# PE's waits put in front of a projection's last matmul, and one ACT copy put ahead of the third exponentials

## The chip, the cores and the metric

The kernel runs on one core of one Trainium2 chip. The metric is the device time of one execution in microseconds (us). Its engines are PE (TensorE, matmuls; PEld is its weight load), DVE (VectorE), ACT (ScalarE), POOL (GpSimd) and SP (SyncE, which issues the DMAs here). Each has its own queue of instructions and waits for the others by semaphores.

## What is computed

A transformer-like block on x of 4 x 512 x 256: a state-space mixer and a gated feed-forward part, each behind a modulated layer norm. The mixer is what matters here; cut to it, the reference is:

```python
proj = u @ W_in.T                                # u: 4 x 512 x 256
xBC, z, A_log = split(proj)                      # x: 256, B and C: 32 heads x 64 each
xBC = causal_conv(xBC, conv_w, 4 taps) + conv_b
x, Bm, Cm = split(xBC)
a = -softplus(A_log)
Lm = exp(segsum(a))                              # 512 x 512 per head, lower triangle
M = einsum('blhn,bshn,bhls->bhls', Cm, Bm, Lm)
y = einsum('bhls,bshp->blhp', M, x) + D * x
out = (y * silu(z + z_bias)) @ W_out.T
```

After it come the gate and residual, the second layer norm, silu(x W1) * (x W3), a Walsh-Hadamard transform folded into W2, and the product with W2.

## The kernel before

The 32 heads are taken in 8 groups of 4, and each group over the 4 batches: 32 steps (g, b). The sequence of 512 is cut into 4 chunks of 128. Inside a chunk M is built directly; between chunks the kernel carries states. A step projects four tiles t = 0 to 3 of 128 channels: t = 0, 1 are B, t = 2, 3 are C (each two pairs of heads). A projection is 6 matmuls of 128 x 512 on the full 128x128 array: weights and inputs are split in a high and a low part, so there are three products (lines 371 to 373) for each of two halves of the depth.

The steps are software-pipelined, and the order on each engine is written out by hand. In PE's step (g, b), b is the batch that is projected, q the step before it, r the step before that:

- `proj` 1 (B of b), `states` of r (48 matmuls of 128x32, line 566), `scores` of r for the second head pair (32 of 64x64, line 547), `b_transposes` of q (3 of 128x128, line 528);
- `proj` 0, `proj` 3, `proj` 2;
- `inter` of r (the earlier states' y parts, 12 matmuls of 128x32, line 583), `intra` of r (the chunk's own y, 32 of 128x32, line 597), `scores` of q for the first pair, `b_transposes` of q for the second.

Each of these helpers holds its semaphore waits at its own head, so the waits for `states` stand behind `proj` 1 and those for `inter` behind `proj` 2.

ACT's step is: copy the states out (line 874), exponentials 0 and 1 of q (line 865, four instructions each), the first tap of the convolution for tiles 1 and 0 out of PSUM (line 831), in batch 3 two casts of the next group's weights (lines 914, 915), exponentials 2, then `b_evacuate(q, 0)` (line 855, which copies the B transposes out of PSUM into b_tok), the taps of tiles 3 and 2, the copy of y (line 880), in batch 3 small coefficient copies (line 931), `b_evacuate(q, 1)` and exponentials 3. In batch 1 a copy (line 940) stands ahead of the exponentials. The taps of tiles 3 and 2 wait for `intra` of r on PE.

DVE's step is six further taps for tiles 1 and 0 (line 1174), the mix (scores times exponentials, line 1162) of q's first pair, six taps for tiles 3 and 2, the mix of the second pair. POOL masks the running sums (line 1475), scales x for the states (line 1448) and splits weights (line 1396). SP loads the running sums (line 234) for each head after the exponentials have used the ones before, and stores y.

Semaphores by name: `taps0` to `taps3` count finished taps of a tile, `bt` transposes, `bt_ev` the copies of line 855 (two a step), `xds_done` the scaled x, `st_copy` the states copied out, `yt_ev` the copy of y, `xs_done` x for `intra`, `mixed` the mixes, `proj0` to `proj3` finished projections. `pe_waits` is only incremented, so that an instruction carries the waits before it. The loop over groups 1 to 7 is a loop on the chip; the steps of group 0 are written out.

Of the kernel before, what the change touches and what calls it, by code (L numbers as in the profile page):

```python
# [19 lines left out]
B, L, D = 4, 512, 256  # L20
# [3 lines left out]
KT = D // P  # L24
# [26 lines left out]
def adaln_ssm_ffn_kernel(nc, u, w_bc, w_x, w_a, w_z, conv, d_rows, z_bias, w_out, w13, w2, c_t, wmod,  # L51
                         consts, out, e_d, gates_d):
    with ExitStack() as ctx:
# [312 lines left out]
        def _(pe):  # L366
# [99 lines left out]

            def proj(g, b, t):
                n = g * B + b
                if isinstance(n, int) and n == 0:
                    pe.wait_ge(s[f"xtaps{t % 2}"], 3 * (3 + t // 2))  # L470
                else:
                    pe.wait_ge(s[f"taps{t}"], 3 * n)
                if b == 0:
                    pe.wait_ge(s["w_split"], g * GT + PLACE[t] + 1)
                for kt in range(KT):
                    i = split_mm(ps[:, PROJ_BANK[t], :], wg_hi[:, t, kt, :], wg_lo[:, t, kt, :],
                                 ht_hi[:, kt, b * L:(b + 1) * L], ht_lo[:, kt, b * L:(b + 1) * L],
                                 kt == 0, kt == KT - 1)
                i.then_inc(s[f"proj{t}"], 1)

# [40 lines left out]
            def b_transposes(q, b, p, first):  # L521
                pe.wait_ge(s[f"taps{p}"], 3 * q + 3)
                if not first or p:
                    pe.wait_ge(s["bt_ev"], 2 * q + p)
                if not first and p == 0:
                    pe.wait_ge(s["st_copy"], 2 * q)
                for c in range(CH - 1):
                    i = nc.tensor.transpose(ps[:, 6, c * P:(c + 1) * P],  # L528
                                            acc[:, b % 2, p, c * P:(c + 1) * P], ident)
                i.then_inc(s["bt"], 1)  # L530

            def scores(q, b, p, first):
# [5 lines left out]
                else:  # L538
                    pe.wait_ge(s["xtok_ev"], 2 * B)
                pe.sem_inc(s["pe_waits"], 1)  # L540
                for c in range(CH):
                    for h in range(2):
# [11 lines left out]
            def states(q, b):  # L554

                pe.wait_ge(s["bt_ev"], 2 * q + 2)
                pe.wait_ge(s["xds_done"], 3 * q + 3)
                pe.sem_inc(s["pe_waits"], 1)
                for p in range(2):
                    for c in range(CH - 1):  # L560
# [11 lines left out]
            def inter(q, b, first):  # L572

                pe.wait_ge(s["st_copy"], 2 * q + 2)
                if first:
                    pe.wait_ge(s["gate_ev"], 1)
                else:
                    pe.wait_ge(s["yt_ev"], q)
                for c in (2, 1, 3):
                    for p in range(2):  # L580
# [5 lines left out]
            def intra(q, b):  # L586

                pe.wait_ge(s["xs_done"], 4 * q + 4)
                pe.wait_ge(s["mixed"], 2 * q + 2)
                for a in range(2):  # L590
                    for h in range(2):
# [34 lines left out]
            def step(g, b, gq, gr):  # L626
# [3 lines left out]
                r = gr * B + br  # L630
                proj(g, b, 1)
                states(r, br)
                scores(r, br, 1, False)
                b_transposes(q, bq, 0, False)
                proj(g, b, 0)
                proj(g, b, 3)
                proj(g, b, 2)
                inter(r, br, isinstance(r, int) and r == 0)
                intra(r, br)
                scores(q, bq, 0, False)  # L640
                b_transposes(q, bq, 1, False)

# [105 lines left out]
        def _(act):  # L748
# [145 lines left out]
            def step(g, b, gq, gr, split=False, last=False):  # L894
# [17 lines left out]
                if split:  # L912
                    act.wait_ge(s["ld_wg"], (g + 2) * 16)
                    nc.scalar.copy(wg_hi[:, 1], wg_raw[:, 1]).then_inc(s["w_high_act"], 1)
                    nc.scalar.copy(wg_hi[:, 0], wg_raw[:, 0]).then_inc(s["w_high_act"], 1)
                decays(q, bq, 2, False)
                b_evacuate(q, 0)
                last_tap(g, b, 3)
# [737 lines left out]
```

## Time and profile before

| | us |
|---|---|
| median of 3 runs | 542.92 (542.3 to 543.33) |
| the profiled execution | 542.52 |
| its span | 540.3 |

| engine | busy, share of the span |
|---|---|
| PE | 529.2 us, 98% |
| PEld | 428.9 us, 79% |
| DVE | 455.4 us, 84% |
| ACT | 373.8 us, 69% |
| POOL | 240.7 us, 45% |

All comes from one profiled execution, with times in us from the start of its span; the granted TensorE clock is 0.999 of full speed over it, that is 2.4 GHz. A matmul's end in the records is modelled and longer than the time for which it holds the array, so distances are read from start to start. An instruction's idle time stands in brackets with what ended it; "issue" means that the profile shows nothing that it waited for. The scan with its 32 steps lies between about 49 and 363 us; before it come the first layer norm and the decays, behind it the feed-forward part.

### The profile page before, as it was taken

How to read it: one execution, taken by the hardware profiler on the slowest of the kernel's cores; microseconds unless marked ns; L12 is line 12 of the kernel's file. 1: busy time of each engine (PE TensorE's matmuls, PEld its weight loads, DVE VectorE, ACT ScalarE, POOL GpSimd, SP SyncE). 2: the span in 40 equal slices, each digit the busy share in tenths (PEclk: the TensorE clock that was granted, in tenths of full speed). 3: DMA queues.
4: the chain of work that ended last, by engine and by line, in shares of the span. 5: the costliest groups of instructions: out<-in, count | busy, mean ns of one | idle time of the engine just before them, and what ended most of it. 6: DMA issues, size and time to landing. Idle time of an engine off the chain costs nothing.

```text
span 540.3 us, 19200 instructions
## 1 busy us (share of the span) xinstructions
PE 529.2 (98%) x7091; PEld 428.9 (79%) x7092; DVE 455.4 (84%) x746; ACT 373.8 (69%) x988; POOL 240.7 (45%) x465
## 2 busy tenths in 40 slices
PE   7899999999999999999999999999999999999997
PEld 4577778878878878878878878876889889889886
DVE  6999999999999999999999999999757657657342
ACT  1878998888898898898898898887534234234240
POOL 6763366676676775776776474374000000000000
PEclk9999999999999999999999999999999999999999
DMA  8737333432423425422422424666521322100101
GB/s 265 279 111 225 111 121 90 138 92 84 139 84 91 139 86 168 139 81 93 138 80 96 137 80 135 168 183 197 170 79 41 78 79 79 39 2 0 40 0 40
DMA packets 50288, 59.38 MB, mean 110 GB/s; under 512 B 8004, under 2 KB 44740, under 8 KB 49864
## 3 DMA queue, kind: packets, MB, share of 16 engines
q1 hardware_dynamic: 50248, 58.88, 35.4%
q8 instruction: 21, 0.34, 0.3%
q14 instruction: 19, 0.16, 0.1%
HBM read 48.75 MB, written 9.05 MB: 107 GB/s over the span
## 4 chain that ended last, share of the span: by engine, by line
PE 87%; DVE 7%; ACT 2%; issue 2%; DMA 1%; POOL 1%; SPq 1%; ACTq 0%; POOLq 0%; DVEq 0%
PE ps L371 20%; PE ps L372 19%; PE ps L373 19%; PE ps L547 9%; PE ps L528 5%; DVE acc L1174 4%; PE ps L597 4%; PE ps L566 3%; PE ps L583 3%; PE ps L664 3%; DMA u_sb<-in_u 1%; PE ps L610 1%; PE ps L674 1%; DVE stats L1050 1%; ACT decay L865 1%
## 5 line engine op out<-in xcount | busy, mean ns | idle before, releaser
L1174 DVE SCALAR_TENSOR_TENSOR acc<-ps,cw_dve,acc 128x511 f32<-128x511 f32 (+2 forms) x384 | 257.9, 742 | 5.1 <-ACT acc L831 4.8
L865 ACT ACTIVATE decay<-sums,p_slot 128x128 f32<-128x128 f32 (+1 forms) x512 | 147.7, 371 | 2.9 <-ACT p_slot L940 1.2
L1475 POOL TENSOR_TENSOR sums<-sums,far_above 128x256 f32<-128x256 f32 x128 | 95.6, 752 | 118.4 <-DMA sums<-packed_sums 112.2
L831 ACT ACTIVATE acc<-ps,cw_act 128x512 f32<-128x512 f32 x128 | 93.1, 777 | 27.3 <-PE ps L597 25.2
L371 PE MATMUL ps<-ht_hi,wg_hi 128*128 128x512 f32 x256 | 107.1, 418 | 0.4 <-POOL wg_lo L1396 0.4
L372 PE MATMUL ps<-ht_lo,wg_hi 128*128 128x512 f32 x256 | 101.2, 395 | 0.0
L373 PE MATMUL ps<-ht_hi,wg_lo 128*128 128x512 f32 x256 | 101.2, 395 | 0.0
L1000 ACT ACTIVATE silu_sb<-ps 128x512 f32<-128x512 f32 x32 | 19.2, 600 | 77.7 <-PE ps L373 77.7
L1162 DVE TENSOR_TENSOR mix<-ps,decay 128x768 f32<-128x768 f32 x64 | 61.0, 954 | 5.6 <-PE ps L547 4.8
L1401 POOL TENSOR_TENSOR rstd<-vareps,minus_half 128x4 f32<-128x4 f32 x8 | 8.4, 1048 | 118.7 <-DVE vareps L1056 116.4
L547 PE MATMUL ps<-acc 64*64 64x128 f32 (+1 forms) x2048 | 57.6, 249 | 0.8
L373 PEld LDWEIGHTS ps<-ht_hi,wg_lo 128*128 128x128 f32 x256 | 48.1, 188 | 11.6
L371 PEld LDWEIGHTS ps<-ht_hi,wg_hi 128*128 128x128 f32 x256 | 48.2, 188 | 10.1 <-POOL wg_lo L1396 0.9
L1313 DVE TENSOR_TENSOR hid<-ps,silu_sb 128x512 f32<-128x512 f32 x32 | 22.1, 692 | 40.4 <-ACT silu_sb L1000 40.3
L372 PEld LDWEIGHTS ps<-ht_lo,wg_hi 128*128 128x128 f32 x256 | 48.5, 189 | 8.4
L547 PEld LDWEIGHTS ps<-acc 64*64 64x64 f32 x2048 | 48.8, 133 | 7.1 <-issue 2.2
L371 PE MATMUL ps<-h_hi,w_hi 128*128 128x512 f32 x128 | 50.5, 394 | 0.0
L373 PE MATMUL ps<-h_hi,w_lo 128*128 128x512 f32 x128 | 49.9, 390 | 0.0
L372 PE MATMUL ps<-h_lo,w_hi 128*128 128x512 f32 x128 | 49.9, 390 | 0.0
L371 PE MATMUL ps<-w_hi,hid_hi 128*128 128x256 f32 x128 | 36.9, 289 | 0.2 <-DVE stage L1329 0.2
L372 PE MATMUL ps<-w_lo,hid_hi 128*128 128x256 f32 x128 | 36.2, 283 | 0.0
L373 PE MATMUL ps<-w_hi,hid_lo 128*128 128x256 f32 x128 | 36.2, 283 | 0.0
(143 smaller groups left out, 892.8 us busy)
## 6 DMA issues: line engine op xcount, KB each, us to landing
sums<-packed_sums SPq DMA_DIRECT2D x256, 96.0 KB, 2.7
wg_raw<-in_w_bc SPq DMA_DIRECT2D x8, 512.0 KB, 4.1
y_parts<-yt_sb SPq DMA_DIRECT2D x64, 64.0 KB, 2.0
stage<-y_parts SPq DMA_DIRECT2D x32, 128.0 KB, 2.8
u_sb<-in_u SPq DMA_DIRECT2D x4, 512.0 KB, 5.0
stage<-in_w SPq DMA_DIRECT2D x1, 2048.0 KB, 14.2
x_channels<-acc SPq DMA_DIRECT2D x8, 256.0 KB, 2.4
ee<-running_sums SPq DMA_DIRECT2D x8, 256.0 KB
```

The source lines that it names most:

```text
L371: mm(o, w_hi, x_hi, start=first, stop=False)
L372: mm(o, w_hi, x_lo, start=False, stop=False)
L373: return mm(o, w_lo, x_hi, start=False, stop=last)
L528: i = nc.tensor.transpose(ps[:, 6, c * P:(c + 1) * P], acc[:, b % 2, p, c * P:(c + 1) * P], ident)
L547: i = mm(ps[NS * at:NS * (at + 1), 2 + a, o:o + P - NS * h], acc[own, b % 2, p, c * P + NS * h:c * P + NS * (h + 1)], acc[own, b % 2, 2 + ...
L597: i = mm(ps[QD * quarter:QD * (quarter + 1), 7, k * P + NS * h:(k + 1) * P], xs[:, b % 2, w:w + QD], mix[:, j, k * PW + NS * (1 - h):k * P ...
L831: af(acc[:, b % 2, t, :], ps[:, PROJ_BANK[t], :], ACT.Identity, bias=cw_act[:, t, 1:2], scale=cw_act[:, t, 0:1]).then_inc(s[f"tap_a{t}"], 1)
L865: i = af(decay[:, j, own], sums[:, j, own], ACT.Exp, scale=-1.0, bias=p_slot[:, b * CH + n, j:j + 1])
L1162: tt(mix[:, 2 * p:2 * p + 2, 0:PL], ps[:, 2:4, 0:PL], decay[:, 2 * p:2 * p + 2, 0:PL], ALU.mult).then_inc(s["mixed"], 1)
L1174: stt(a[:, d:], ps[:, PROJ_BANK[t], 0:L - d], cw_dve[:, t, TAPS - 1 - d:TAPS - d], a[:, d:], ALU.mult, ALU.add).then_inc(s[f"taps{t}"], 1)
L1313: tt(hid[:, m % 2, :], ps[:, 2 + m % 2, :], silu_sb[:, m % 2, :], ALU.mult).then_inc(s["hid_done"], 1)
L1475: gp.tensor_tensor(v, v, far, ALU.add).then_inc(s["masked"], 1)
```

## The change

On PE, `proj` is cut in two: `proj_start` issues the waits of the projection and its first five matmuls, `proj_end` the sixth. In the steps that have r and q (all but the first two), the waits that stood at the heads of `states`, of the first `scores` (without `mixed`) and of the first `b_transposes` (without `st_copy`) now stand between `proj_start(g, b, 1)` and `proj_end(b, 1)`; of those of `inter`, `intra`, the second `scores` and the second `b_transposes` all that are not implied by others stand between `proj_start(g, b, 2)` and `proj_end(b, 2)`. The matmuls, their order and their operands stay; so do the conditions, each of which is waited for no later in the queue than before. Two increments of `pe_waits` a step go. On ACT, `b_evacuate(q, 0)` moves from behind to ahead of the exponentials 2. The first two steps and the stretch after the loop keep the old form.

```diff
-            def proj(g, b, t):
+            def proj_start(g, b, t):
...
-                for kt in range(KT):
-                    i = split_mm(ps[:, PROJ_BANK[t], :], wg_hi[:, t, kt, :], wg_lo[:, t, kt, :],
-                                 ht_hi[:, kt, b * L:(b + 1) * L], ht_lo[:, kt, b * L:(b + 1) * L],
-                                 kt == 0, kt == KT - 1)
-                i.then_inc(s[f"proj{t}"], 1)
+                o, own = ps[:, PROJ_BANK[t], :], slice(b * L, (b + 1) * L)
+                split_mm(o, wg_hi[:, t, 0, :], wg_lo[:, t, 0, :], ht_hi[:, 0, own], ht_lo[:, 0, own], True, False)
+                mm(o, wg_hi[:, t, 1, :], ht_hi[:, 1, own], start=False, stop=False)
+                mm(o, wg_hi[:, t, 1, :], ht_lo[:, 1, own], start=False, stop=False)
+
+            def proj_end(b, t):
+
+                own = slice(b * L, (b + 1) * L)
+                mm(ps[:, PROJ_BANK[t], :], wg_lo[:, t, 1, :], ht_hi[:, 1, own], start=False,
+                   stop=True).then_inc(s[f"proj{t}"], 1)
...
-                proj(g, b, 1)
-                states(r, br)
-                scores(r, br, 1, False)
-                b_transposes(q, bq, 0, False)
+                proj_start(g, b, 1)
+                pe.wait_ge(s["xds_done"], 3 * r + 3)
+                pe.wait_ge(s["taps3"], 3 * r + 3)
+                pe.wait_ge(s["taps1"], 3 * r + 3)
+                pe.wait_ge(s["taps0"], 3 * q + 3)
+                pe.wait_ge(s["bt_ev"], 2 * r + 2)
+                proj_end(b, 1)
+                states_now(br)
+                pe.wait_ge(s["mixed"], 2 * r + 1)
+                pe.sem_inc(s["pe_waits"], 1)
+                scores_now(br, 1)
+                pe.wait_ge(s["st_copy"], 2 * r + 2)
+                b_transposes_now(bq, 0)
                 proj(g, b, 0)
                 proj(g, b, 3)
-                proj(g, b, 2)
-                inter(r, br, isinstance(r, int) and r == 0)
-                intra(r, br)
-                scores(q, bq, 0, False)
-                b_transposes(q, bq, 1, False)
+                proj_start(g, b, 2)
+                if isinstance(r, int) and r == 0:
+                    pe.wait_ge(s["gate_ev"], 1)
+                else:
+                    pe.wait_ge(s["yt_ev"], r)
+                pe.wait_ge(s["xs_done"], 4 * r + 4)
+                pe.wait_ge(s["taps2"], 3 * q + 3)
+                pe.wait_ge(s["taps1"], 3 * q + 3)
+                pe.wait_ge(s["mixed"], 2 * r + 2)
+                pe.wait_ge(s["bt_ev"], 2 * q + 1)
+                proj_end(b, 2)
+                inter_now(br)
+                intra_now(br)
+                scores_now(bq, 0)
+                b_transposes_now(bq, 1)
...
+                b_evacuate(q, 0)
                 decays(q, bq, 2, False)
-                b_evacuate(q, 0)
                 last_tap(g, b, 3)
```

## Rows read from the trace of the kernel before

**Rows 1.** The page, part 1: busy us (share of the span) and instructions.

```profile
PE 529.2 (98%) x7091; PEld 428.9 (79%) x7092; DVE 455.4 (84%) x746; ACT 373.8 (69%) x988; POOL 240.7 (45%) x465
```

**Rows 2.** Timeline of PE and PEld, batch 3: start, duration, instruction, count, [idle before].

```profile
311.37 0.40 PE L373 MATMUL ps<-ht_hi,wg_lo 128*128 128x512 f32 x1
317.49 0.39 PE L373 MATMUL ps<-ht_hi,wg_lo 128*128 128x512 f32 x1
...
311.14 0.19 PEld L373 LDWEIGHTS ps<-ht_hi,wg_lo 128*128 128x128 f32 x1
311.70 0.51 PEld L566 LDWEIGHTS ps<-xds,b_tok 128*32 128x32 f32 x48 [0.37 <-issue]
317.81 0.25 PEld L583 LDWEIGHTS ps<-acc,st_sb 128*32 128x32 f32 x10 [0.36 <-issue]
```

**Rows 3.** Line 589's wait, and timeline of PEld at other changes of work.

```profile
L589 PEldq EVENT_SEMAPHORE  x2: 51/51/51, 316.4 to 326.6; - x2
...
27.38 0.14 PEld L423 LDWEIGHTS ps<-h,wa_sb 128*32 128x32 f32 x4 [0.36 <-issue]
...
54.36 0.48 PEld L528 LDWEIGHTS ps<-cst,acc 128*128 128x128 f32 x3
```

**Rows 4.** Timeline of ACT's second b_tok copies, and PE in the first step.

```profile
310.74 0.50 ACT L855 COPY b_tok<-ps 128x384 f32<-128x384 f32 x1
320.88 0.50 ACT L855 COPY b_tok<-ps 128x384 f32<-128x384 f32 x1
58.59 0.48 ACT L855 COPY b_tok<-ps 128x384 f32<-128x384 f32 x1
...
58.93 0.40 PE L373 MATMUL ps<-ht_hi,wg_lo 128*128 128x512 f32 x1
```

**Rows 5.** Timeline of two copies on ACT and the weight loads that waited for them.

```profile
332.99 0.20 ACT L874 COPY st_sb<-ps 64x48 f32<-64x48 f32 x1
333.31 0.31 PEld L528 LDWEIGHTS ps<-cst,acc 128*128 128x128 f32 x3
...
80.47 0.43 ACT L874 COPY st_sb<-ps 64x48 f32<-64x48 f32 x2 [0.19 <-PE ps L566]
81.08 0.20 PEld L528 LDWEIGHTS ps<-cst,acc 128*128 128x128 f32 x2
```

**Rows 6.** Timeline of PE and PEld in a step of batch 0.

```profile
320.14 0.19 PEld L371 LDWEIGHTS ps<-ht_hi,wg_hi 128*128 128x128 f32 x1
320.48 0.39 PE L372 MATMUL ps<-ht_lo,wg_hi 128*128 128x512 f32 x1
321.41 0.40 PE L373 MATMUL ps<-ht_hi,wg_lo 128*128 128x512 f32 x1
321.73 0.51 PEld L566 LDWEIGHTS ps<-xds,b_tok 128*32 128x32 f32 x48 [0.37 <-issue]
322.39 0.69 PEld L547 LDWEIGHTS ps<-acc 64*64 64x64 f32 x30
```

**Rows 7.** Timeline of ACT's third exponentials, and of projection 2's last matmul on PE.

```profile
317.12 1.18 ACT L865 ACTIVATE decay<-sums,p_slot 128x128 f32<-128x128 f32 x4
75.49 1.18 ACT L865 ACTIVATE decay<-sums,p_slot 128x128 f32<-128x128 f32 x4
75.06 0.39 PE L373 MATMUL ps<-ht_hi,wg_lo 128*128 128x512 f32 x1
296.89 1.17 ACT L865 ACTIVATE decay<-sums,p_slot 128x128 f32<-128x128 f32 x4
297.42 0.39 PE L373 MATMUL ps<-ht_hi,wg_lo 128*128 128x512 f32 x1
```

**Rows 8.** Timeline of PE where a projection starts late.

```profile
77.98 0.50 PE L371 MATMUL ps<-ht_hi,wg_hi 128*128 128x512 f32 x1
118.95 0.51 PE L371 MATMUL ps<-ht_hi,wg_hi 128*128 128x512 f32 x1 [0.39 <-POOL wg_lo L1396]
```

**Rows 9.** Timeline of DVE's taps of tiles 1 and 0.

```profile
305.98 4.02 DVE L1174 SCALAR_TENSOR_TENSOR acc<-ps,cw_dve,acc 128x511 f32<-128x511 f32 x6
```

More of the change, by code:

```diff
@@ L474, in proj @@
                     pe.wait_ge(s["w_split"], g * GT + PLACE[t] + 1)
-                for kt in range(KT):
-                    i = split_mm(ps[:, PROJ_BANK[t], :], wg_hi[:, t, kt, :], wg_lo[:, t, kt, :],
-                                 ht_hi[:, kt, b * L:(b + 1) * L], ht_lo[:, kt, b * L:(b + 1) * L],
-                                 kt == 0, kt == KT - 1)
-                i.then_inc(s[f"proj{t}"], 1)
+                o, own = ps[:, PROJ_BANK[t], :], slice(b * L, (b + 1) * L)
[6 more added lines that the diff above has]
+                   stop=True).then_inc(s[f"proj{t}"], 1)
+            def proj(g, b, t):
+                proj_start(g, b, t)
+                proj_end(b, t)
             pe.wait_ge(s["zero_set"], 1)
@@ L526, in b_transposes, with b_transposes_now @@
                     pe.wait_ge(s["st_copy"], 2 * q)
+                b_transposes_now(b, p)
+            def b_transposes_now(b, p):
                 for c in range(CH - 1):
@@ L540, in scores, with scores_now @@
                 pe.sem_inc(s["pe_waits"], 1)
+                scores_now(b, p)
+            def scores_now(b, p):
                 for c in range(CH):
@@ L558, in states, with states_now @@
                 pe.sem_inc(s["pe_waits"], 1)
+                states_now(b)
+            def states_now(b):
                 for p in range(2):
@@ L578, in inter, with inter_now @@
                     pe.wait_ge(s["yt_ev"], q)
+                inter_now(b)
+            def inter_now(b):
                 for c in (2, 1, 3):
@@ L589, in intra, with intra_now @@
                 pe.wait_ge(s["mixed"], 2 * q + 2)
+                intra_now(b)
+            def intra_now(b):
                 for a in range(2):
```

## The prediction

> **What bounds the kernel now.** I read the page's busy shares first: PE is busy for 98% of the span, DVE for 84%, ACT for 69% [rows 1]. PE sets the pace, so I went to the timeline of PE and its weight loads in the middle of the scan, where one step (one group of heads, one batch) takes 10.03 us: the loads of the states begin at 311.70 and again at 321.73 [rows 2, 6]. Inside a projection a long matmul starts every 0.23 us, and its weights are loaded beside the matmul before it: those of the matmul of 311.37 from 311.14 on [rows 2]. At two places of a step this breaks. After the last matmul of projection 1 the states' load starts 0.33 us later, and after the last of projection 2 (317.49) the load for the earlier states' y parts 0.32 us later, each with 0.36 or 0.37 us of idle time marked "issue" [rows 2]. So some 0.09 us lies open twice a step. With 30 steps that have states, at most 0.09 x 60 = 5.4 us could come back there.
>
> **Is that opening the price of the waits?** I say no, by two readings. One: the wait on line 589, which stands before the y parts, was executed at 316.4, over 1 us before 317.81, and the opening is there all the same [rows 2, 3]. Two: before the B transposes of 54.36 stands a wait as well, yet their load carries no idle mark; they use the full 128x128 array, as the projections do. The loads of 128x32 at 27.38 have one wait in front and carry the mark of 0.36 us, the same as the states with two waits and a semaphore increment [rows 2, 3]. The opening goes with the change from the full array to a part of it, and that stays. So I book no gain, with 5.4 us as the other bound. The Trainium skill (TensorEngine Tiling (Array Packing), Key Properties) says that a change of tiling mode drains TensorE. By that rule too the opening stays and the sum is as below; without it the sum would be 5.4 us lower. The rows on both shapes agree with it, though none shows the drain itself.
>
> **What the moved waits ask for.** In front of the last projection matmul they must be met 0.3 to 0.6 us sooner. Most are early: DVE has finished the taps of the batch before at 305.98 + 4.02 = 310.00, needed at 311.14 [rows 2, 9]; the second mix, POOL's scaled x and the y copy of the batch before are earlier by 1 us or more, and cost nothing. Two are late, and both are ACT's copy of transposes to b_tok. Queued behind the waiting load on PE is everything: the last projection matmul, states, scores, transposes. ACT's last tap waits for that matmul, DVE's taps and mix for ACT. A delay isn't won back on ACT, whose next copy hangs on taps that wait for the end of PE's y parts.
>
> **The price of a late wait.** From the end of a copy on ACT to the load that waits for it: 332.99 + 0.20 = 333.19 to 333.31, so 0.12 us [rows 5]. From a load that nothing covered to streaming: the load starts at 320.14, the second matmul after it is recorded at 320.48, and the first must have begun to stream 0.23 us before that, at 320.25: 0.11 us [rows 6]. Together 0.23 us from the end of the copy. The bounds: the copy that ended at 80.47 + 0.43 = 80.90 was followed by its load at 81.08, 0.18 instead of 0.12, which makes 0.29; and if the weights were in the array already, 0.12 alone is left [rows 5].
>
> **Part A, the waits before projection 1's last matmul.** The copy begun at 310.74 ends at 311.24; that matmul can stream at 311.47 instead of 311.37, 0.10 us late [rows 2, 4]. Of the 30 steps 22 are of this kind: 2.2 us. In steps of batch 0 ACT has one small copy more before it (line 931) and ends at 320.88 + 0.50 = 321.38, so 321.61 instead of 321.41: 0.20 us, five times, and once 0.10: 1.1 us; the seventh is held by weights before that and pays nothing [rows 4, 6]. These seven give something back. Scores follow states after 0.66 us there (321.73 to 322.39), 0.10 more than in other steps, because three waits are handled between them after a late release, and two of the three move forward: 0.7 us off [rows 6]. The first step costs 58.59 + 0.48 + 0.23 = 59.30 against 58.93: 0.37 us [rows 4]. Semaphore increments dropped I take as nothing; PE's queue hides them. A = 2.2 + 1.1 - 0.7 + 0.4 = 3.0 us.
>
> **Part B, the waits before projection 2's last matmul, with ACT's moved copy.** The copy now starts where the third exponentials started, and takes 0.46 to 0.48 us, so streaming is possible 0.69 us after that start. In steps of batches 0 and 2 the start is early enough by 0.27 us or more, and that is nothing. Batch 3: two weight casts (lines 914, 915) stand ahead on ACT, in seven steps: 317.12 + 0.69 = 317.81 against 317.49, 0.32 us, five times, so 1.6 us; where ACT had also waited for POOL, 75.49 + 0.69 = 76.18 against 75.06, 1.12 us; once 0.46 us. Together 3.2 us [rows 2, 7]. Batch 1: a copy (line 940) stands ahead: 296.89 + 0.69 = 297.58 against 297.42, 0.16 us, five like it 0.8 us and two others 0.3 us: 1.1 us [rows 7]. B = 4.3 us. The exponentials come 0.38 us later. What hides that is ACT's idle time before its next tap, 0.5 to 1.1 us in most steps; without it up to 0.4 us a step would go to DVE's taps.
>
> **What swallows part of it.** In the step before 120 PE already waits 0.39 us for POOL's weight split at 118.95, and about as much again in starting up; that hides the 0.32 of the step before. At 77.98 PE starts a projection some 0.25 us late, held by DVE, which hides as much of the 1.12 [rows 8]. The last step of the scan is bound by DVE: 0.1. Together 0.7 us.
>
> **The sum.** 3.0 + 4.3 - 0.7 = 6.6 us. The profiled execution took 542.52 us (span 540.3 and 2.2 around it), so 549.1 for one like it. It stands 0.4 under the median of the runs, 542.92, which becomes 549.5.
>
> **Rivals.**
> - *Stalls dearer.* In other steps too the blocked sequencer falls behind, and short matmuls after it start late, as in batch 0 by 0.10 us [rows 6]. Against it: the release is followed by one long matmul, which gives it time. In 23 steps and at 14 places of part B: 37 x 0.10 = 3.7 more, 553.2.
> - *The openings were the waits', the stalls as priced.* For it: the page calls them "issue" [rows 2]. Against it: the two readings. 549.5 - 5.4 = 544.1.
> - *Faster.* The openings go, and a held last matmul has its weights in already, so a late wait costs 0.12 and not 0.23. Part A: 0.3 for the first step, 5 x 0.09 for batch 0, less 0.7: 0. Part B: 5 x 0.21 + 1.01 + 0.35 + 0.4 = 2.8. Sum 0 + 2.8 - 0.5 - 5.4 = -3.1: 539.8. The place is the pair of openings in each step; it decides once they return more per step than the two stalls take. Against it: the loads that waited for a copy start only after its end [rows 5].
> - *It does not bite.* The copies land in time, because ACT gains elsewhere, and nothing opens or closes: 542.9. For it: the margins are a tenth of a us. Against it: ACT's time is tied to PE's.
>
> **How the numbers follow.** Forecast 0.62, stalls dearer 0.10, openings gone with the stalls as priced 0.13, faster 0.07, no effect 0.08. Bounds of the forecast: 43 stalls (29 in A, 14 in B), each by 0.06 more or 0.10 less: 545.2 to 552.1. To leave out no more than 2 in 10 the range takes in the first two rivals: 543.8 to 553.2. About 0.2%, or 1.1 us, is what a measurement of this kernel can tell from no change. The second rival ends at that bound and is split. Faster 0.08, same 0.12, slower 0.80.
>
> **What would show it.** Right: the idle marks before states and y parts stay at 0.32 to 0.37 us; the last weight load of projection 1 starts 0.12 us after ACT's b_tok copy ends and no longer beside its forerunner; from the states of batch 3 to the next states 10.5 us, from batch 2's to batch 3's 10.13. Wrong: states 0.23 us after the last long matmul, steps of 10.03 us as before, or the copy of line 855 ending well ahead of the last matmul of projection 1 or 2.

## The result, and the profile after

| kernel | median (lowest to highest) | runs |
|---|---|---|
| before | 542.52 us (541.85 to 543.54) | 9 |
| changed | 546.27 us (544.55 to 548.52) | 9 |

The ratio is 1.0072, with an interval of 1.0058 to 1.0086: slower by 3.75 us, where 6.6 were forecast. The profiled execution of the changed kernel has a span of 543.8 us, 3.5 more than before.

The page after, part 1 (engines) and the row of the granted clock of part 2. They answer [rows 1].

```profile
PE 533.5 (98%) x7092; PEld 429.1 (79%) x7092; DVE 455.8 (84%) x746; ACT 373.2 (69%) x988; POOL 240.6 (44%) x465
PEclk9899999999999999999999999999999999999999
```

DVE, ACT and POOL do what they did; only PE's busy time moves, by 4.3 us. The 8 near the start is a dip of the clock ahead of the scan that some executions of a kernel show and others don't, so stretches are compared here and not only spans.

In the changed kernel the last projection matmul is line 483, states 585, scores 563, y parts 605 (`inter`) and 622 (`intra`), the b_tok copy 899. The waits by engine and line after: us in total, times, longest.

```profile
PEld ps L483 <- ACT b_tok L899: 10.8, 40, 0.6
PEld ps L605 <- issue: 9.9, 32, 0.6
PEld ps L585 <- issue: 7.7, 31, 0.4
```

The first line is the new wait: 40 of some 60 last matmuls are held by ACT's copy, as forecast (43). The 10.8 us are idle time of the weight loader, not of the array: a load may stand late and still lie beside the matmul before it. The two other lines are the openings, which are still there.

Timeline after of PEld, PE and ACT, steps of batches 2 and 3. They answer [rows 2, 4, 7]. A view marks idle time from 0.15 us on.

```profile
309.48 0.19 PEld L478 LDWEIGHTS ps<-ht_lo,wg_hi 128*128 128x128 f32 x1
309.72 0.19 PEld L483 LDWEIGHTS ps<-ht_hi,wg_lo 128*128 128x128 f32 x1
310.27 0.26 PEld L605 LDWEIGHTS ps<-acc,st_sb 128*32 128x32 f32 x10 [0.36 <-issue]
...
313.79 0.19 PEld L483 LDWEIGHTS ps<-ht_hi,wg_lo 128*128 128x128 f32 x1 [0.19 <-ACT b_tok L899]
314.21 0.51 PEld L585 LDWEIGHTS ps<-xds,b_tok 128*32 128x32 f32 x48 [0.24 <-issue]
...
320.15 0.19 PEld L483 LDWEIGHTS ps<-ht_hi,wg_lo 128*128 128x128 f32 x1 [0.48 <-ACT b_tok L899]
320.57 0.25 PEld L605 LDWEIGHTS ps<-acc,st_sb 128*32 128x32 f32 x10 [0.24 <-issue]
...
324.19 0.19 PEld L483 LDWEIGHTS ps<-ht_hi,wg_lo 128*128 128x128 f32 x1 [0.28 <-ACT b_tok L899]
324.61 0.51 PEld L585 LDWEIGHTS ps<-xds,b_tok 128*32 128x32 f32 x48 [0.24 <-issue]
...
313.64 0.40 PE L478 MATMUL ps<-ht_lo,wg_hi 128*128 128x512 f32 x1
313.87 0.42 PE L483 MATMUL ps<-ht_hi,wg_lo 128*128 128x512 f32 x1
314.22 0.60 PE L585 MATMUL ps<-xds,b_tok 128*32 128x24 f32 x48
...
319.71 0.39 PE L478 MATMUL ps<-ht_lo,wg_hi 128*128 128x512 f32 x1
...
313.24 0.50 ACT L899 COPY b_tok<-ps 128x384 f32<-128x384 f32 x1
...
319.01 0.40 ACT L958 CAST wg_hi<-wg_raw 128x256 fp32r<-128x256 f32 x1
319.62 0.48 ACT L899 COPY b_tok<-ps 128x384 f32<-128x384 f32 x1
...
323.64 0.50 ACT L899 COPY b_tok<-ps 128x384 f32<-128x384 f32 x1
```

Three kinds of place are to be seen. At 309.72 (projection 2, batch 2) nothing is late: the load stands 0.24 behind its forerunner, as in a plain projection. At 313.79 (projection 1) the copy ended at 313.74 and the load follows it by 0.05 us, early enough to lie beside the matmul of 313.64, which streams until 313.87; the last matmul's record is at 313.87, and PE loses nearly nothing. At 320.15 (projection 2, batch 3) the matmul before ended its streaming at 319.94, the load has no cover, and the y parts come at 320.57 instead of 320.26.

A step is best read from states to states. The medians over the steps of one batch, worked out from the first record of each of the 32 groups of states, and the means, which hold the irregular steps too:

| from the states in the step that projects batch | 0 | 1 | 2 | 3 |
|---|---|---|---|---|
| steps | 7 | 7 | 8 | 8 |
| before, median (mean) | 10.13 (10.13) | 10.03 (10.05) | 10.03 (10.04) | 10.05 (10.37) |
| after, median (mean) | 10.03 (10.03) | 10.13 (10.15) | 9.99 (10.00) | 10.49 (10.68) |

By the means, 7 x -0.10 + 7 x 0.10 + 8 x -0.03 + 8 x 0.31 = 2.2 us. Half of the steps are shorter than before, which the forecast had nowhere; the loss is in the column of batch 3. A stretch runs into the next step, so that column holds what projection 1 of batch 0 loses too.

The rest of the 3.5 us lies outside. The first states wait for ACT's first copy; and behind the scan stands a gap that before does not have. Timeline after, ACT and PEld, in the first step, and PEld at the y parts of the tail; the last line is before's tail:

```profile
58.77 0.50 ACT L899 COPY b_tok<-ps 128x384 f32<-128x384 f32 x1
59.38 0.19 PEld L483 LDWEIGHTS ps<-ht_hi,wg_lo 128*128 128x128 f32 x1 [0.53 <-issue]
59.81 0.51 PEld L585 LDWEIGHTS ps<-xds,b_tok 128*32 128x32 f32 x48 [0.24 <-issue]
...
380.15 0.36 PEld L605 LDWEIGHTS ps<-acc,st_sb 128*32 128x32 f32 x10
381.09 0.14 PEld L605 LDWEIGHTS ps<-acc,st_sb 128*32 128x32 f32 x2 [0.58 <-issue]
...
377.38 0.36 PEld L583 LDWEIGHTS ps<-acc,st_sb 128*32 128x32 f32 x12
```

From the end of the first copy to the first states it is 59.81 - 59.27 = 0.54 us; before, the copy of 58.59 ended at 59.07 [rows 4] and the states came at 59.26, 0.19: 0.35 more. In the tail, 12 loads that need no wait between them stand in a row at 377.38 in before; after, they break behind the tenth for 0.58 us.

All kernels in one table, by stretches of their traces. The middle one, from the first states to the last, is the scan without its first step. The last, from the last states to the span's end, holds the break. Each ratio is taken to runs of before from the same round, whose medians are 542.39 to 542.76, so it can differ a little from the quotient of the times shown.

| kernel | us, median | ratio to before (interval) | first states at | scan | behind it |
|---|---|---|---|---|---|
| before | 542.52 | | 59.26 | 315.41 | 165.6 |
| changed | 546.27 | 1.0072 (1.0058 to 1.0086) | 59.81 | 317.59 | 166.4 |
| e1_a_only | 542.17 | 0.9995 (0.9985 to 1.0004) | 59.61 | 314.37 | 166.7 |
| e2_b_only | 546.81 | 1.0077 (1.0061 to 1.0093) | 61.07 | 317.64 | 166.1 |
| e3_bt_behind | 541.92 | 0.9985 (0.9971 to 0.9999) | 60.26 | 313.58 | 167.0 |
| e4_act_old | 573.32 | 1.0566 (1.0540 to 1.0591) | 60.07 | 344.65 | 166.0 |
| e5_casts_behind | 543.73 | 1.0018 (1.0006 to 1.0029) | 59.03 | 315.18 | 166.6 |
| e6_taps_only | 540.87 | 0.9965 (0.9954 to 0.9976) | 59.44 | 312.95 | 165.7 |
| e7_bt_behind_pad | 542.37 | 1.0001 (0.9991 to 1.0011) | 61.74 | 312.61 | 165.6 |
| e8_transposes_first | 544.77 | 1.0048 (1.0028 to 1.0068) | 60.80 | 317.69 | 165.5 |
| e9_bt_first | 548.81 | 1.0105 (1.0090 to 1.0120) | 59.83 | 320.83 | 166.1 |

### The profile page after: what moved, and what is told of

It is laid out like the page before. It is cut to its first block, busy times and chain, and to the rows that moved or that the text cites. A ratio compares the mean times of both kernels' runs of the same rounds, so it can differ in the third digit from the quotient of the medians.

```text
span 543.8 us, 19055 instructions
## 1 busy us (share of the span) xinstructions
PE 533.5 (98%) x7092; PEld 429.1 (79%) x7092; DVE 455.8 (84%) x746; ACT 373.2 (69%) x988; POOL 240.6 (44%) x465
## 4 chain that ended last, share of the span: by engine, by line
PE 88%; ACT 4%; DVE 4%; issue 2%; DMA 1%; POOL 0%; SPq 0%; ACTq 0%; DVEq 0%; POOLq 0%
PE ps L371 15%; PE ps L372 14%; PE ps L373 14%; PE ps L563 8%; PE ps L483 6%; PE ps L541 5%; PE ps L478 5%; PE ps L477 5%; PE ps L622 4%; PE ps L585 3%; PE ps L605 3%; PE ps L708 3%; DVE acc L1218 2%; ACT decay L909 1%; DMA sums<-packed_sums 1%
## 5 line engine op out<-in xcount | busy, mean ns | idle before, releaser
L483 PE MATMUL ps<-ht_hi,wg_lo 128*128 128x512 f32 x128 | 53.1, 415 | 1.2 <-ACT b_tok L899 0.7
L373 PE MATMUL ps<-ht_hi,wg_lo 128*128 128x512 f32 x128 | 50.5, 394 | 0.0
L483 PEld LDWEIGHTS ps<-ht_hi,wg_lo 128*128 128x128 f32 x128 | 24.1, 188 | 16.4 <-ACT b_tok L899 10.8
```

Of the source, the lines that this page charges most:

```text
L373: return mm(o, w_lo, x_hi, start=False, stop=last)
L483: mm(ps[:, PROJ_BANK[t], :], wg_lo[:, t, 1, :], ht_hi[:, 1, own], start=False, stop=True).then_inc(s[f"proj{t}"], 1)
```

## The experiments

**The two halves, each alone (e1, e2).** e1 changes projection 1's group only and leaves ACT as before:

```diff
-                proj(g, b, 1)
-                states(r, br)
-                scores(r, br, 1, False)
-                b_transposes(q, bq, 0, False)
+                proj_start(g, b, 1)
+                pe.wait_ge(s["xds_done"], 3 * r + 3)
+                pe.wait_ge(s["taps3"], 3 * r + 3)
+                pe.wait_ge(s["taps1"], 3 * r + 3)
+                pe.wait_ge(s["taps0"], 3 * q + 3)
+                pe.wait_ge(s["bt_ev"], 2 * r + 2)
+                proj_end(b, 1)
...
                 proj(g, b, 2)
                 inter(r, br, isinstance(r, int) and r == 0)
```

e2 is the reverse: projection 2's group and ACT's moved copy as in the change, projection 1's group as before.

> Only the first half of PE's change: the waits before states, the first scores and the first B transposes stand before the last matmul of projection 1; projection 2 and ACT's order are as in the kernel before. Late-copy theory, priced from the trace of the changed kernel: in ordinary steps the last matmul's load starts 0.05 us after the copy to b_tok and costs the step 0.02 us, while the scores follow the states 0.05 us sooner; batch 0 loses 0.13 and gets 0.11 back, the first step loses 0.3. Sum about -0.4, so 542.1 beside 542.5, no measurable change. Rival, part A as the prediction had it (0.10 a step, 3.0 in all): 545.5. Rival, the openings were the waits': states 0.23 us after the last long matmul, 3 us less.

> Only the second half: the waits before the y parts stand before the last matmul of projection 2 and ACT copies the transposes ahead of the third exponentials; projection 1 as before. Late-copy theory: batch 3 loses 0.32 us five times, 0.45 once and about 0.9 once, batch 1 loses 0.13 five times and 0.3 once: +4.0, so 546.5, nearly all of the change's loss. Rival, the loss is spread over both halves as predicted (4.3 minus 0.6 here, 3.0 in the other): 546.2 here and 545.5 for the other half. Rival, a general slowing by the longer wait list: batches 0 and 2 would lose too.

Waits of e1, then of e2 (the line of the b_tok copy is 889 and 890 in them):

```profile
PEld ps L483 <- ACT b_tok L889: 5.9, 28, 0.3
...
PEld ps L483 <- ACT b_tok L890: 4.6, 13, 0.6
```

e1 holds 28 loads, each for a short time, and costs nothing: 0.9995. e2 holds 13, and is as slow as the whole change. Its batches 1 and 3 take 10.12 and 10.38 us (medians), the others 10.12 and 10.03 as before. So the loss is the second half's. By the medians of the runs the halves add up: 0.9995 x 1.0077 = 1.0072. In the traces, of which there is one for each kernel, they don't quite: in the scan e1 is 1.04 us shorter than before, and the changed kernel is 3.22 longer than e1, while e2 is 2.23 longer than before. Irregular steps make much of that difference of 1.0. In the first step of batch 3, where POOL holds ACT, it is 0.46: 10.29 us in before and 10.62 in e2, but 10.09 in e1 and 10.88 after. The second step of batch 3 adds 0.57 and the last takes 0.52 off again. That the second half has less to hide behind where the first has removed a hold-up would explain the first two; no run shows it.

**Only the b_tok waits behind, ACT as before (e3).** From the changed kernel:

```diff
-                pe.wait_ge(s["bt_ev"], 2 * r + 2)
                 proj_end(b, 1)
+                pe.wait_ge(s["bt_ev"], 2 * r + 2)
                 states_now(br)
...
-                pe.wait_ge(s["bt_ev"], 2 * q + 1)
                 proj_end(b, 2)
                 inter_now(br)
                 intra_now(br)
                 scores_now(bq, 0)
+                pe.wait_ge(s["bt_ev"], 2 * q + 1)
                 b_transposes_now(bq, 1)
...
-                b_evacuate(q, 0)
                 decays(q, bq, 2, False)
+                b_evacuate(q, 0)
```

> The change without the two waits for b_tok copies: they stand behind the projections again, one directly before states, one before the second B transposes, and ACT has its old order; all other waits stay moved. Late-copy theory: no load of a last matmul waits any more; what stays is the return between states and scores, 0.05 us in 22 steps and 0.11 in 7: -2.0, so 540.5, faster than both kernels. The openings before states and y parts stay at 0.32 to 0.33 us, before the y parts with no wait at all in between. Rival, openings due to waits: 3 to 5 us less, 537 to 540. Rival, the moved waits themselves cost: 544 or more.

The scan is 1.83 us shorter than before, but the time only 0.6 (540.5 was expected). PEld in e3's tail:

```profile
376.62 0.36 PEld L605 LDWEIGHTS ps<-acc,st_sb 128*32 128x32 f32 x11
378.19 0.11 PEld L605 LDWEIGHTS ps<-acc,st_sb 128*32 128x32 f32 x1 [1.22 <-issue]
```

The break took the gain: 1.22 us, now behind the eleventh load. The y parts, which in this kernel have no wait and no increment between them and the last long matmul, still come 0.32 us behind it (0.318 to 0.325 in all 30 steps). All waits that are met in time cost nothing; the two b_tok waits are the loss.

**The break moved away (e7).** e3 with 48 increments of `pe_waits` more on PE ahead of the scan. Nothing in the scan or in the tail is different.

```diff
             norm_transposes(0)
+            for _ in range(24):
+                pe.sem_inc(s["pe_waits"], 1)
...
             norm_transposes(2)
+            for _ in range(24):
+                pe.sem_inc(s["pe_waits"], 1)
```

> The version with the b_tok waits left behind the projections, and 48 semaphore increments on PE in two idle stretches of the first layer norm, so that the code behind the scan lies where it lay in the kernel before. Theory of code loading: the break of 0.4 to 1.2 us among the twelve y-part matmuls behind the scan goes, and the scan's 1.8 us reach the end: 540.7. Rival, the break has another cause (data or PSUM): 541.9 as without them, or a little more for the increments.

PEld in e7's tail:

```profile
377.11 0.36 PEld L609 LDWEIGHTS ps<-acc,st_sb 128*32 128x32 f32 x12
```

The break is gone, and behind the scan the trace has 165.6 us, as before. The time was a miss, 542.37 for 540.7, and alone it would speak for the rival: the padding stands in front of work of PE, and in e7's trace the scan's first long matmul comes at 41.34 instead of 39.11 us, with the clock's dip in that stretch. In the traces of e2, e3, e4, e8 and e9, which have the dip and no padding, it comes at 39.43 to 40.43, which leaves 0.9 to 1.9 us for the padding, an estimate.

What the run shows is that the break hangs on where the instructions stand in PE's program. The other kernels say it more sharply. Counted in the compiled programs, where each y part is two instructions, a load and a matmul:

| kernel | PE's program, instructions more or less than before's | the break stands ahead of | idle, us |
|---|---|---|---|
| e1 | -10 | load 3 of 12 | 1.07 |
| e2 | -12 | load 4 | 0.51 |
| e9 | -23 | matmul 9, load 10 | 0.54 |
| after, e4, e5 | -26 | load 11 | 0.58, 0.40, 0.85 |
| e3 | -28 | load 12 | 1.22 |
| e6, e8, before, e7 | -6, -3, 0, +20 | no break | |

In all seven traces with a break it falls on the same place of the program. In e1, for one, the y parts begin 10 instructions sooner than in before and four of them stand ahead of load 3, so the break lies 6 instructions ahead of where before's y parts begin; 12 - 6, 26 - 20, 28 - 22, and 23 - 17 for e9's matmul 9, give 6 as well. In e6 that place is the first y part, in the three others it lies among the scores.

And the traces show what arrives there. The page has a DMA queue for instructions, q8, with 21 packets, 0.34 MB; that is about the size of PE's program (348 KB) in pieces of 16 KB. In each of the seven a piece landed 1.25 to 1.48 us before the break ended (after: landed at 379.75, the break ended at 381.09; e3: 376.79 and 378.19). In the four without a break the same piece had landed 2.8 to 3.5 us before the first y part (before: 373.93 for 377.38; e7: 373.98 for 377.11). So in the break PE waits for the next piece of its program, by all that the timing can tell. Why the piece starts 3.9 to 4.7 us before the first y part in the four, and only 1.0 to 2.0 us before it once the program is 10 or more instructions shorter, isn't shown.

**ACT's order (e4).** The changed kernel with `b_evacuate(q, 0)` back behind `decays(q, bq, 2, False)`.

```diff
-                b_evacuate(q, 0)
                 decays(q, bq, 2, False)
+                b_evacuate(q, 0)
```

> PE's part of the change whole, but ACT copies the transposes behind the third exponentials as before. Late-copy theory: the last load of projection 2 starts 0.05 us after the end of that copy in every step, some 0.7 us late in batches 0 and 2, 1.1 in batch 1 and 1.3 in batch 3: about +25, 566 to 572. Rival, ACT's move is not what the time hangs on: 546.

The wait of e4, and ACT and PEld in its timeline:

```profile
PEld ps L483 <- ACT b_tok L899: 39.3, 56, 1.7
...
310.08 0.46 ACT L899 COPY b_tok<-ps 128x384 f32<-128x384 f32 x1
310.60 0.19 PEld L483 LDWEIGHTS ps<-ht_hi,wg_lo 128*128 128x128 f32 x1 [0.96 <-ACT b_tok L899]
```

27.1 us more in the scan than after, 0.9 a step, and a time just above the 566 to 572 that were expected: without the moved copy every step's last matmul of projection 2 waits for four exponentials. Nearly nothing of a late copy is won back elsewhere, since ACT's next taps wait for PE in turn: in batch 3 the last matmul of projection 2 and the y parts behind it come 1.37 us late (1.50 us behind the matmul before, and 0.42 behind the record, for 0.23 and 0.32), and the step takes 11.45 us instead of before's 10.05, 1.40 more. That is the loop that the forecast assumed.

**The casts of batch 3 (e5).** The changed kernel with the copy ahead of the two weight casts too:

```diff
+                b_evacuate(q, 0)
                 if split:
                     act.wait_ge(s["ld_wg"], (g + 2) * 16)
                     nc.scalar.copy(wg_hi[:, 1], wg_raw[:, 1]).then_inc(s["w_high_act"], 1)
                     nc.scalar.copy(wg_hi[:, 0], wg_raw[:, 0]).then_inc(s["w_high_act"], 1)
-                b_evacuate(q, 0)
                 decays(q, bq, 2, False)
```

> The changed kernel with one more move on ACT: in batch 3 the two weight casts stand behind the copy to b_tok instead of ahead of it. Late-copy theory: the copy starts 0.6 us sooner in batch 3, so the last matmul of projection 2 is no longer held there (0.32 us five times, 0.45 and up to 0.9 once): 2.5 to 3 less than the changed kernel, 543.5 beside 542.5 for the kernel before; batch 1 keeps its 0.13. Rival, the loss comes from the list of waits as such: 546 as the changed kernel.

ACT and PEld of e5 in a step of batch 3:

```profile
316.13 0.48 ACT L899 COPY b_tok<-ps 128x384 f32<-128x384 f32 x1
316.49 0.42 ACT L959 CAST wg_hi<-wg_raw 128x256 fp32r<-128x256 f32 x1
...
316.82 0.19 PEld L483 LDWEIGHTS ps<-ht_hi,wg_lo 128*128 128x128 f32 x1
317.37 0.25 PEld L605 LDWEIGHTS ps<-acc,st_sb 128*32 128x32 f32 x10 [0.36 <-issue]
```

The load is no longer held, and batch 3 takes 10.09 us (median) instead of 10.49. The scan is 2.4 us shorter than after's: two casts ahead of one copy were most of the loss, 2.5 of 3.75 us by the medians of the runs.

**Is the opening the change of array shape? (e8).** In before, the B transposes, which use the full array as the projection does, are put directly behind projection 1, ahead of states and scores:

```diff
                 proj(g, b, 1)
+                if not (isinstance(r, int) and r == 0):
+                    pe.wait_ge(s["st_copy"], 2 * r)
+                b_transposes(q, bq, 0, True)
                 states(r, br)
                 scores(r, br, 1, False)
-                b_transposes(q, bq, 0, False)
```

> The kernel before with one order changed on PE: the first B transposes, on the full array, stand directly behind projection 1, and states and scores behind them; the waits in front of the transposes are three, one of them the late copy to b_tok. Array-shape theory: the transposes' load starts beside or within 0.05 us of the end of the last long matmul (0.23 to 0.28 us after its start, no idle mark or a small one), and the opening moves to between transposes and states. Rival, waits make the opening: the transposes start 0.33 us or more after the last long matmul, as states did. The time itself within 2 us of the kernel before.

PEld and PE of e8 behind projection 1 (line 373 is its last matmul, 528 the transposes, 566 the states):

```profile
314.11 0.19 PEld L373 LDWEIGHTS ps<-ht_hi,wg_lo 128*128 128x128 f32 x1
314.34 0.48 PEld L528 LDWEIGHTS ps<-cst,acc 128*128 128x128 f32 x3
314.99 0.51 PEld L566 LDWEIGHTS ps<-xds,b_tok 128*32 128x32 f32 x48 [0.17 <-issue]
...
314.34 0.39 PE L373 MATMUL ps<-ht_hi,wg_lo 128*128 128x512 f32 x1
314.57 0.49 PE L528 MATMUL ps<-cst,acc 128*128 128x128 f32 x3
```

Behind the same projection, with three waits in front of them, the transposes' load starts beside the last long matmul, with no idle mark, and their first matmul follows at the plain 0.23 us. The mark has moved to the states, where the shape changes now. With e3, where no wait is left and the opening stays, that settles it: the opening goes with the shape. It agrees with the rule of the Trainium skill that a change of tiling mode drains TensorE (TensorEngine Tiling (Array Packing), Key Properties); the price, some 0.09 us from a matmul of 512 columns on the full array to 128x32, is this trace's. Behind short matmuls a change of shape shows less: the loads lie 0.05 to 0.09 us apart from states to scores, from y parts to scores and from scores to transposes, and 0.17 from transposes to states here. The kernel as a whole is slower by 0.5%, or 2.2 us, a little more than the 2 expected; the likely reason is that ACT's copies of the states now come later (e8's waits have ACT idle for states for 16.7 us, before's for 2.9), which no run separates.

**The price of a late wait, by its place in the group (e9).** The changed kernel with the late wait first of the five in projection 1's group instead of last:

```diff
                 proj_start(g, b, 1)
+                pe.wait_ge(s["bt_ev"], 2 * r + 2)
                 pe.wait_ge(s["xds_done"], 3 * r + 3)
                 pe.wait_ge(s["taps3"], 3 * r + 3)
                 pe.wait_ge(s["taps1"], 3 * r + 3)
                 pe.wait_ge(s["taps0"], 3 * q + 3)
-                pe.wait_ge(s["bt_ev"], 2 * r + 2)
                 proj_end(b, 1)
```

> The changed kernel with one change of order: in front of the last matmul of projection 1 the late wait (for ACT's copy to b_tok) stands first of the five waits, the four early ones behind it; in the changed kernel it is the last and rides on the weight load. Theory that the handling of the waits makes the price: behind the release the sequencer must still go through the others, so the load starts 0.12 us or more after the copy instead of 0.05, the states come that much later in 29 steps: 2 to 6 us more than the changed kernel, 548.5 to 552. Rival, a release costs the same wherever the wait stands: 546.3 as the changed kernel.

ACT and PEld of e9, an ordinary step, then one of batch 0:

```profile
315.96 0.50 ACT L899 COPY b_tok<-ps 128x384 f32<-128x384 f32 x1
316.59 0.19 PEld L483 LDWEIGHTS ps<-ht_hi,wg_lo 128*128 128x128 f32 x1 [0.26 <-issue]
...
326.43 0.50 ACT L899 COPY b_tok<-ps 128x384 f32<-128x384 f32 x1
327.27 0.19 PEld L483 LDWEIGHTS ps<-ht_hi,wg_lo 128*128 128x128 f32 x1 [0.56 <-issue]
```

The load now starts 0.12 us after the copy's end in the one (the rows are rounded) and 0.34 in the other, where the changed kernel has 0.05 in both. Nothing else differs between the kernels, and the scan is 3.2 us longer, 0.11 a step. The rows of PE's queue by line show why. Line 661 is the group's last wait, 526 in before the wait for the states' copy ahead of the transposes; each row of its own has count, duration in ns and time. First before around 333 [rows 5], then after in the first step, then after and e9 in an ordinary step, then e9 in batch 0:

```profile
L526 PEldq EVENT_SEMAPHORE  x1: 51/51/51, 333.2 to 333.2; - x1
...
L661 PEldq EVENT_SEMAPHORE  x1: 51/51/51, 59.3 to 59.3; - x1
...
L661 PEldq ALU_OP  x1: 32/32/32, 312.6 to 312.6; - x1
...
L661 PEldq ALU_OP  x1: 32/32/32, 316.5 to 316.5; - x1
...
L658 PEldq FUSED_REGOPS  x1: 37/37/37, 327.0 to 327.0; - x1
L660 PEldq EVENT_SEMAPHORE  x1: 51/51/51, 327.1 to 327.1; - x1
L661 PEldq FUSED_REGOPS  x1: 56/56/56, 327.2 to 327.2; - x1
```

In an ordinary step after, the last wait has no semaphore instruction of its own; only its value is worked out, at 312.6, a whole us before the copy's end at 313.74, and the load can go 0.05 us after it. In e9 the small instructions of the waits behind stand between the release (316.46 and 326.93) and the load. In the first step after, and before the transposes of before, the wait is an instruction of its own of 51 ns that comes after the release (59.27; 333.19): these are the places with 0.11 and 0.12 us. So the price of a late wait on PE is what is still to be handled behind it: nothing 0.05 us, its own instruction 0.11 to 0.12, one register instruction 0.12, several 0.34.

It is the order in PE's queue that counts, and that need not be the order in kernel.py. In the two written-out steps of group 0 it is the other way round: in the changed kernel, with the late wait last in kernel.py, it became an instruction of its own and the load follows the copy by 0.11 us; in e9, with the late wait first, the load carries it and follows by 0.05.

**Only what is early (e6).** Before, with just the three waits for taps moved ahead of projection 1's last matmul. Every other wait stays at its old place or is implied by one that stands before it, and ACT is as before:

```diff
-                proj(g, b, 1)
-                states(r, br)
-                scores(r, br, 1, False)
-                b_transposes(q, bq, 0, False)
+                proj_start(g, b, 1)
+                pe.wait_ge(s["taps3"], 3 * r + 3)
+                pe.wait_ge(s["taps1"], 3 * r + 3)
+                pe.wait_ge(s["taps0"], 3 * q + 3)
+                proj_end(b, 1)
+                pe.wait_ge(s["bt_ev"], 2 * r + 2)
+                pe.wait_ge(s["xds_done"], 3 * r + 3)
+                pe.sem_inc(s["pe_waits"], 1)
+                states_now(br)
+                pe.wait_ge(s["mixed"], 2 * r + 1)
+                pe.sem_inc(s["pe_waits"], 1)
+                scores_now(br, 1)
+                pe.wait_ge(s["st_copy"], 2 * r + 2)
+                b_transposes_now(bq, 0)
```

> The kernel before with only the waits for taps moved ahead of the last matmul of projection 1 (three waits that are met 1 us and more before); all else as before. Theory of the return: scores follow states after 0.53 instead of 0.59 us, and 0.57 instead of 0.68 in batch 0, 2.0 us over the scan; behind the scan 0.4 to 1.2 us go at the earlier states' y parts, as in every version so far whose code on PE is shorter: 541.3. Rival, what the first half of the change returned came from waiting longer in front of states, not from fewer waits behind them: 542.4.

PEld of e6, an ordinary step, then the y parts of its tail:

```profile
309.79 0.51 PEld L585 LDWEIGHTS ps<-xds,b_tok 128*32 128x32 f32 x48 [0.37 <-issue]
310.32 0.75 PEld L563 LDWEIGHTS ps<-acc 64*64 64x64 f32 x32
...
375.15 0.36 PEld L605 LDWEIGHTS ps<-acc,st_sb 128*32 128x32 f32 x12
```

540.87 us, faster than both kernels; the interval of its ratio lies below 1. The opening of 0.37 is as before, since the waits weren't it. But by the matmul records the scores follow the states 0.53 us later and no longer 0.59, and in batch 0 0.57 instead of 0.68: between the short matmuls of the states and those of the scores two waits fewer are handled (`taps1` and `taps3`; the wait for `mixed` and the increment stay). 23 x 0.054 + 7 x 0.11 = 2.0 us of the 2.46 that the scan gained. The expectation had a break of 0.4 to 1.2 us in the tail, and there is none; the time came out below the 541.3 that went with it.

## Why the forecast was right in its direction and too high in its size

**The openings.** Right: they stay, also where no wait and no increment is left between the last long matmul and the next work (309.72 to 310.27 after, e3, e6), and e8 moved them with the shape. One reading behind it was put wrongly: line 589 is the wait of `intra`, behind the first y parts in the program; of their own waits the one with a record, line 578, had been executed earlier still, at 315.2. The bound of 5.4 us had no part in the result. The mark before the states after a held load is 0.24 instead of 0.37, but that is no gain: the load ahead of it stands later by as much.

**Which waits are late.** Right: the two b_tok copies and no other. e3 and e6 lose nothing with all others moved, and e4 shows that a delay there isn't won back.

**Part B.** Nearly right: 4.3 less 0.7, so 3.6 forecast; on top of the first half it measures 3.22 (317.59 - 314.37), without it 2.23 (e2). Four of the ordinary steps of batch 3 take 10.40 to 10.42 us where e1 has 10.09 (median), so 0.32, as forecast; batch 1 takes 10.13 where e1 has 10.00, so 0.13, forecast 0.16; batches 0 and 2 lose nothing. The step with POOL loses 0.79 (10.88 against e1's 10.09), forecast 1.12 less 0.25. The 0.32 came out with two errors that cancel. An uncovered late load costs 0.05 + 0.10 = 0.15 us from the copy's end (320.10, 320.15, and y parts 0.42 instead of 0.32 behind the record) and not 0.23, which would give 0.08 less. And the copy's start stood nearer to PE's matmul, 319.62 for 319.94, than 317.12 for 317.49 in [rows 7], which gives 0.05 back.

**Part A.** Here the sum failed: forecast 3.0, measured -1.04 in the scan and +0.35 in the first step, -0.7. Two terms were mis-sized.
- *The price of a late wait*, 0.12 from the copy to the load and 0.11 from the load to streaming [rows 5, 6]. The first was read from a load whose wait is an instruction of its own (line 526, above); the moved one of projection 1 (line 661) has none in 28 of its 30 places, and measures 0.05. It holds in the first step, where there is one: 0.35 lost, forecast 0.37. The second was read from a load that nothing covered; here the copy is so little late that the load still lies beside the matmul before it. From the copy's end to the states it was 311.24 to 311.70 = 0.46, and is 313.74 to 314.22 = 0.48: 0.02 and not 0.10, 1.8 us less over 22 steps. In batch 0 it is 0.13 and not 0.20 (before 321.38 to 321.73, after 324.14 to 324.61, with means over its steps behind the 0.13), 0.4 us less.
- *The two waits that leave the place between states and scores.* The forecast booked what they return in the seven steps of batch 0 only, 0.7, which came as forecast (0.11 x 7 = 0.77). In the 23 others it had nothing for them, and they return 0.054 each, 1.2 us. The increments that it took as nothing are not the cause: e6 keeps them all and returns the same 0.054.

3.0 - 1.8 - 0.4 - 1.2 = -0.4, against the measured -0.7.

**What was in no step.** The break in the tail, 0.58 us idle and 0.8 in that stretch. And 0.2 us ahead of the first states, which differs from execution to execution. So the span: 0.55 (first states 59.81 for 59.26, 0.35 of it the first copy's) + 2.18 + 0.8 = 3.5 us.

The direction thus rests on part B alone, and some luck is in the size: part A came out with the other sign, and the break, which no term had, brought the time 0.8 us nearer to the forecast.

**The rivals.** *Stalls dearer* falls: after a release, states and scores follow no later than before, and the stalls were cheaper. *The openings were the waits', stalls as priced* (544.1) falls by e8 and e3, though by the time alone it did better than the forecast: the measured 3.75 us lie nearer to its 1.2 (6.6 - 5.4) than to 6.6. *Faster* had its mechanism wrong, since no opening went, but one half of it, a late wait cheaper than 0.23 us, was right. *It does not bite* falls by the 40 held loads. The signs named ahead came out in part: the idle marks before y parts whose last matmul was not held stayed at 0.36, and the stretch from the states of batch 3 to the next is 10.49 us in the median (10.5 named); but the load followed the copy by 0.05 and not 0.12, and batch 2's stretch to batch 3's is 9.99 and not 10.13.

**What stays open.** Why the piece of PE's program comes so late in the tail of seven of the kernels; whether the two halves together lose 1.0 us more than each alone, as the single traces have it, or add up, as the medians of the runs do; and how much of e7's late start is its padding.

## What to carry to other kernels

Move a wait ahead of long work only if its release is already there at that point. Here three early waits moved gave -0.35%, and the two late ones turned the same idea into +0.7%. What moving waits gains lies between two dense groups of short matmuls, where a wait costs its handling, and not behind a long matmul, where the idle mark belongs to the change of array shape. Where a late wait can't be avoided, let it be the last that PE's queue handles ahead of the load, and read that from the trace: in the loop it was the last wait of its group in kernel.py, in the written-out steps the first. Ahead of blaming an edit for a few tenths of a per cent, compare the traces by stretches: a gap far from the edit can come from the program having another length, as the break of 0.4 to 1.2 us did here.

## What the runs showed of the hardware that was not expected

- A weight load started 0.05 us after the ACT copy that it waited for when nothing was left to handle, 0.11 to 0.12 where the wait was an instruction of its own, and 0.12 to 0.34 when the other waits' register instructions stood between.
- A late weight load cost PE next to nothing as long as it still lay beside the streaming of the matmul before (0.02 us a step), and about 0.10 us once it didn't (y parts 0.42 instead of 0.32 us behind the record of the last matmul).
- Two waits fewer between 48 matmuls of 128x32 and 32 of 64x64 let the second group start 0.054 us sooner, 0.11 where the first group's release had been late.
- Twelve dense short matmuls in the tail were broken by 0.40 to 1.22 us in seven of the traces (changed kernel, e1 to e5, e9) and not in before, e6, e7 and e8; 48 instructions more, far ahead of it, made the break go. It fell on the same instruction of PE's program in all seven, and ended 1.25 to 1.48 us after a 16 KB packet of the instruction queue had landed.
- The stretch ahead of the scan, in which all kernels but e7 are alike, differed by up to 1.9 us between the traces (first long matmul at 38.54 to 40.43), with the granted clock's dip in some of them.
